# Local attention on one core: ScalarE computes the logarithm and exponential of the norms before the square, in each step

## The reference

```
qkv = h @ wqkv                              # h: tokens, half of the channels shifted by one
q, k = l2norm(q) * q_scale, l2norm(k) * k_scale
q, k = rotary_xpos(q, k)                    # x*cos*scale + rotate_half(x)*sin*scale
sim  = (8*q) @ k.T   within windows of 64 and the window before, masked
out  = softmax(sim) @ v
x    = x + concat(out) @ wo
```

## Time and profile before

| | |
|---|---|
| median of 3 runs | 2303.07 us (2303.02 to 2311.46) |
| the profiled execution, own time | 2294.92 us |
| its span, first to last instruction | 2293.1 us |
| mean granted TensorE clock | 0.978 |
| busy, share of the span | PE 93%, ACT 79%, DVE 74%, PEld 69%, POOL 62% |
| local attention, from the first to the last L295 | 741.8 to 994.0, 1085.2 to 1337.4, 1606.9 to 1860.2, 1951.6 to 2205.1 us |
| share of the span in these four | 1011 of 2293 us, 44% |

### The profile page before, as it was taken

How to read it: one execution, slowest core, us unless ns; L and a number is a source line. 1 busy time by engine, 2 the same in 40 slices (tenths; PEclk the granted TensorE clock), 3 DMA queues, 4 the chain that set the end, 5 groups by cost and what they waited for, 6 DMA issues and landing times. The chain is left out here.

```text
span 2293.1 us, 67424 instructions
## 1 busy us (share of the span) xinstructions
PE 2136.7 (93%) x22342; PEld 1585.6 (69%) x22342; DVE 1706.8 (74%) x4362; ACT 1801.0 (79%) x6112; POOL 1431.8 (62%) x1432
## 2 busy tenths in 40 slices
PE   6997999998797999999999999898999999999999
PEld 4994666665795888854888854674788864788863
DVE  5565999996555899964899964675899963899964
ACT  4775999995676999973999973556999982999982
POOL 3663777774662888840888850671788850788850
PEclk8997999999899999999999999999999999999999
DMA  6111000000113000000000000000000000000000
GB/s 249 44 42 42 2 0 0 0 1 38 35 44 111 12 7 9 7 3 3 11 7 9 7 0 0 2 0 6 9 9 8 8 1 5 9 9 7 9 1 37
DMA packets 22568, 46.02 MB, mean 20 GB/s; under 512 B 5344, under 2 KB 13664, under 8 KB 22048
## 3 DMA queue, kind: packets, MB, share of 16 engines
q1 hardware_dynamic: 17440, 34.07, 4.4%
q0 software_dynamic: 4992, 10.23, 1.6%
HBM read 24.51 MB, written 11.40 MB: 16 GB/s over the span
## 5 line engine op out<-in xcount | busy, mean ns | idle before, releaser
L280 POOL TENSOR_TENSOR space<-space 128x512 f32<-128x512 f32 x256 | 325.8, 1273 | 270.4 <-DVE space L383 270.1
L275 POOL TENSOR_TENSOR space<-space 128x512 f32<-128x512 f32 x256 | 267.6, 1045 | 128.1 <-ACT space L316 127.6
L330 ACT ACTIVATE space<-psum,space 128x128 f32<-128x128 f32 x1024 | 337.0, 385 | 2.7 <-DVE space L374 2.7
L177 PE MATMUL psum<-big,space 128*128 128x256 f32 x1024 | 267.9, 384 | 7.3 <-issue 3.5
L269 POOL TENSOR_TENSOR space<-space 128x512 f32<-128x512 f32 x256 | 267.0, 1043 | 7.9 <-DVE space L354 7.3
L1008 POOL TENSOR_TENSOR space<-space 128x256 f32<-128x256 f32 (+1 forms) x256 | 221.9, 888 | 75.2 <-DVE space L1117 70.9
L374 DVE TENSOR_REDUCE space<-psum 128x4 f32<-128x512 f32 x256 | 177.1, 692 | 100.8 <-PE psum L192 96.5
L1053 ACT ACTIVATE space<-space 128x128 f32<-128x128 f32 (+1 forms) x512 | 226.1, 446 | 7.3 <-DVE space L1108 6.5
L330 ACT ACTIVATION_READ_ACCUMULATOR space<-psum,space 128x1 f32 x1024 | 201.8, 197 | 0.0
L177 PEld LDWEIGHTS psum<-big,space 128*128 128x128 f32 x1024 | 175.6, 191 | 29.6 <-issue 16.2
L677 ACT ACTIVATE big<-psum,wt 128x512 f32<-128x512 f32 (+1 forms) x96 | 65.4, 686 | 151.9 <-PE psum L654 151.9
(11 more groups left out here) (194 smaller groups left out, 5425.8 us busy)
## 6 DMA issues: line engine op xcount, KB each, us to landing
big<-early SPq DMA_DIRECT2D x1, 6944.0 KB, 27.9
rows<-space SPq DMA_DIRECT2D x16, 256.0 KB, 2.7
z<-token_y SPq DMA_DIRECT2D x16, 256.0 KB, 4.7
space<-z SPq DMA_DIRECT2D x64, 64.0 KB, 1.9
space<-z SPq DMA_DIRECT2D x64, 63.8 KB, 2.1
big<-late SPq DMA_DIRECT2D x1, 3114.0 KB, 13.7
x<-x_t SPq DMA_DIRECT2D x4, 512.0 KB, 6.0
x_final<-x SPq DMA_DIRECT2D x8, 256.0 KB, 2.0
```

What stands on the lines that cost most here:

```text
L177: ins = mm(qk_ps[:, t * T:(t + 1) * T].rearrange("p (n c) -> p n c", n=2), hT[:, k, t * P:(t + 1) * P], wq[:, 0:2, j, :], start=(t == 0), ...
L275: pool.tensor_tensor(x, x, rn[:, (j - 1) % 2, :].unsqueeze(2).to_broadcast([P, 8, LD]), ALU.mult).then_inc(scaled, 1)
L280: pool.tensor_tensor(t3[:, j % 2, :], t1[:, j % 2, :], t2[:, j % 2, :], ALU.add).then_inc(summed, 1)
L330: ins = act.activation(pr[:, j % 2, h, t * P:(t + 1) * P], s_ps[h][:, t * P:(t + 1) * P], ACT.Exp, bias=nm[:, j % 2, h, t:t + 1], accum_ou ...
```

## The change

In `scalar_body` the block that computes the reciprocal norm of unit s-1 (the wait for ss_ready, Ln, the wait for ln_ready and for `scaled` of two units before, Exp) goes from behind the square of unit s to ahead of it. The condition becomes `only is None and ...`, since it now stands ahead of the early exit for `only`. No instruction is added or removed, and no buffer, semaphore or other engine's program changes. In the new file the lines are: Ln L305, Exp L309, the square L314.

```diff
L381 TENSOR_TENSOR space<-psum,tabs 128x512 [waits att_summed,att_sq_ready]
L383 TENSOR_TENSOR space<-psum,tabs 128x512
L391 TENSOR_TENSOR space<-psum,space 128x256 [waits att_wo_ready,att_o0_ready]
L354 RECIPROCAL space<-psum 128x4 [waits att_normed,att_p_ready]
L360 CAST psum<-cb 128x2x256
L366 TENSOR_REDUCE space<-space 128x8 [waits att_ln_ready,att_sq_ready]
L374 TENSOR_REDUCE space<-psum 128x4 [waits att_s_ready]IFF
```

More of the change, by code:

```diff
@@ L301, in scalar_body @@
                 act.activation(pt[:, j % 2, :, :].rearrange("p h n -> p (h n)"), pt_ps, ACT.Copy).then_inc(pt_ready, 1)
+            u = s - 1
+            if only is None and runs(u, U):
+                act.wait_ge(ss_ready, S0 + u + 1)
+                act.activation(lnn[:, (j - 1) % 2, :], ss[:, (j - 1) % 2, :], ACT.Ln, scale=float(2 ** 20), bias=g.tiny[:, 0:1]).then_inc(ln_ready, 1)
+                act.wait_ge(ln_ready, S0 + u + 1)
+                if at_least(u, 2):
+                    act.wait_ge(scaled, S0 + u - 1)
+                act.activation(rn[:, (j - 1) % 2, :], lnn[:, (j - 1) % 2, :], ACT.Exp, scale=-0.5, bias=g.tiny[:, 1:2]).then_inc(rn_ready, 1)
             if begins(s, only):
@@ L308, in scalar_body @@
                 continue
[L309 to L316, removed]
             u = s - 4
```

## The result

The changed kernel takes 2330.23 us, median of 4 runs (2329.06 to 2331.49), against 2304.39 us for the kernel before (4 runs): a ratio of 1.0106, 95% interval 1.0084 to 1.0128. It is slower by 26 us; 2334 was forecast, and 2330 lies inside its range of 2317 to 2352. The profiled execution took 2329.12 us with a span of 2327.3 us, at a mean granted clock of 0.979.

The account below looks back on a forecast made before the run. Loop A, 3.97 us, bound ordinary steps; with the change loop B and Loop C at 4.10 do, +0.13 a step. 240 x 0.13 = 31 us on 2303 gives 2334 us, range 2317 to 2352.

Parts of the forecast that it names:

- Loop A: Cycle POOL L275, PE L255, ACT L295, L301, square, Ln, Exp, L275: 3.97 us, said to bind the old step.
- loop B: Cycle ACT L330, DVE L354, L360, L366, ACT Ln, Exp, L322, L330: 3.62 us before, 4.10 with the square.
- Loop C: New cycle DVE L366, ACT Ln, Exp, square, DVE L381, L383, L391, L354, L360, L366: 4.10 us.
- The unknown (1): Whether ACT's square can start 0.21 us after the blocked Exp; extra delay taken as 0, upper bound 0.09 us.
- The rival that rested on it: Slower by more: the square starts 0.09 us late, a step costs +0.22, time 2356 us; 7 in 100.
- Steps with j = 0: One step in four, where register instructions carry a wait: 0.08 to 0.17 us in four steps.
- Faster: Rival: Ln's wait for L366 doesn't feed back, step falls to ACT's own pace, 3.85 us; 2274 us, 6 in 100.
- No change: Rival: ACT does the same work and the reordering only shifts its idle spots; 2303 us, 9 in 100.
- ACT's own pace: Sum of the distances between ACT's starts in one local-attention step, put at 3.85 us.
- the late projection L177: PE's projection waits for DVE L383, 0.2 us of cover left; if late, only the next square, with 0.8 us, follows.

Follow-up runs that it names:

- e4: Kernel before, with POOL's multiplication L275 on half of each head's columns: ratio 0.9832 to the kernel before.
- e3: Changed kernel, with POOL's multiplication L275 on half of each head's columns: ratio 1.0114 to the kernel before.
- e9: Changed kernel, with DVE's addition L391 made in four pieces of 64 columns: ratio 1.0289 to the kernel before.
- e1: Changed kernel, with DVE's sum of squares L366 on half of each head's columns: ratio 0.9856 to the kernel before.
- e5: Changed kernel, with the square one place later, behind the copy L322: ratio 1.0547 to the kernel before.

## Why the prediction was right

- **What bound before.** Loop A, summed to the step's 3.97. e4 shows it: L275 0.43 us shorter, step down to the next limit at 3.85, and e3 shows that this holds only in the old order.
- **What the change puts in its place.** 4.10 was summed for loop B from rows in which it had 0.35 us of slack; measured 4.09. Term by term: L330 to the last read's end 1.38 (1.39), to L354 0.04 (0.03), to L366 0.68 (0.68), its time 0.67, to Ln 0.03 (0.04), to Exp 0.34, to the square 0.20 (0.21), to L322 0.48, to L330 0.27 (0.26). Loop C, 4.10 in the sum, is 4.09 too; there two terms were off and cancel: the square's time is 0.58 for 0.60, and L391 to L354, which was inferred as 0.33, is 0.35.
- **The unknown (1)**, whether the square can start 0.21 us after a blocked Exp with its register instruction and its wait between: it starts 0.20 after (932.69 to 932.89). The rival that rested on it fell.
- **Steps with j = 0.** Before, two of four steps are 4.04 instead of 3.97, which is the two register instructions on loop A. For the changed kernel 0.08 to 0.17 us per four steps was the bound; the series of L295's starts has one step of 4.26 in four, +0.17, the upper end: the other steps inside a stage stay between 4.08 and 4.13, but for one in each of the first two local attentions, of 4.33 and 4.32 us, which I leave open. In e9, where only C binds, the step with j = 0 is 4.34 against 4.26, +0.08. So the two register instructions cost what was said, on the loops that were said.
- **Sum.** 29.0 us in the four stages, 26 in the medians, against 31. The small difference is the factor: I kept 0.13 a step where my own sum gave 0.12; the mean is 29.0 / 252 = 0.115. Some luck is in that. Steps with j = 0 cost 0.01 more than the 0.03 a step that was put for them, and one step in eight, the length of the loop's body, takes another 0.1 us or more before the change (4.14 to 4.28) and at most 0.04 in the changed kernel (4.13, but for the two of 4.33 and 4.32, each the first of its row), which no term of the prediction has. That is 0.01 to 0.02 a step the other way; what makes it is not followed here.
- **"Faster" fell** on e1: it needed L366 not to feed back, and L366 is exactly what the step hangs on. **"No change"**, also what the Trainium skill's rule would give (Perfetto Trace Analysis, Identifying the Most-Contended Engine), fell on the ratio: ACT's occupancy, 97% before, went down while the time went up. By e4 ACT's own pace of about 3.77 was 0.2 us below what bound, and PE's of 3.85 was 0.12 below.
- The Trainium skill's figure for the square (ScalarE: Activation LUTs, What ACT_TABLE_LOAD costs) would have given 0.52 us from the square to L322; it is 0.48 here as before the change (932.89 to 933.37), and with 0.04 more the step would have been 4.13.
- **What was wrong.** The 3.85 us in the rival "Faster" were called ACT's own pace, with 0.38 from L337 to L295. That distance held a wait for PE; it is 0.30 without one. That the next limit came out at 3.85 all the same is luck: it is PE's. I also said the waits would list ACT for L366, with 0.1 us or more of idle ahead of Ln. The gap is there (L301 ends at 932.21, Ln starts at 932.35), but the view lists it in 17 of 64 steps only. And of the late projection L177 I said that only the next square would suffer. It is held up now: PE reaches it early, and it begins at 930.76, 0.06 us after L383's end at 930.70, as PE's timeline of the same step shows. But behind it on PE stand L192 and L209. In the changed kernel that costs nothing, since L192 then starts 0.14 us after the mask is written (931.89 against 931.75) and DVE waits for the square longer than for that; in e5 it is one of the two ways by which the late square holds up L192.

```profile
930.32 0.60 PE L255 MATMUL psum<-cf,space 128*128 128x128 f32 x4
930.76 1.13 PE L177 MATMUL psum<-big,space 128*128 128x256 f32 x4
931.89 0.67 PE L192 MATMUL psum<-space 64*64 64x64 f32 x20
```

## What to carry to other kernels

In a pipeline written by hand the step is the longest loop through queues and semaphores, and an engine at 97% may still not be the bound, nor even the next one. Before an operation is moved, write down every loop through its old and its new place, with the slack of each: a move takes an operation's time out of the loops that cross its old place and puts it into those that cross the new one, and here 0.48 us went from a loop at 3.97 into one at 3.62, and made a second one of 4.09 that had not been there. Where an instruction must wait for its predecessor's result on the same engine, that hole is the cheapest place to put another; and of an operation that becomes late, name all that stands behind it in its queue.

## What was not expected of the hardware

- An addition of 128x256 on DVE, one input in PSUM, took 0.35 us from start to start; in four pieces of 128x64 it took 0.53, so a piece costs 0.13 and the split only 0.06 us for each further one. I had put 0.10.
- An ACT operation's shown duration depends on what it follows. L295 shows 597 ns where it waits for PE, and 667 ns (the middle value of the changed kernel) where it follows L337 at once, with the distance to L301 the same, 0.48 to 0.49 us. Durations are thus not to be summed; distances between starts are, as long as nothing waited between them. The 597 ns in e1 and e4 are the sign that L295 waits for PE there.
